# Node table of a two-layer graph network: 24 of 49 row blocks written by indirect scatters from GpSimd instead of by the sync queue's stores

## What is computed

```python
h = x @ W1 + b1                                        # layer 0
e = concatenate([h[dst], h[src] - h[dst]], axis=-1)
m = relu(relu(e @ W2 + b2) @ W3 + b3)
x = layernorm(x + relu(segment_max(m, dst, num_segments=N)))
AX = segment_sum(edge_weight[:, None] * x[src], dst, num_segments=N)   # layer 1
x = layernorm(x + AX @ W.T + b)
```

## Time and profile before

| what | value |
|---|---|
| runs | 2743.94, 2748.93, 2750.56 us |
| median | 2748.93 us |
| span of the profiled execution (first to last instruction) | 2717.3 us |
| what lies between this span and the median | 31.6 us |
| POOL busy in the span | 2132.2 us (78%) |
| TensorE busy | 1719.5 us (63%) |
| DVE, ScalarE busy | 1267.4, 1128.0 us |

### The profile page before, as it was taken

The page is one execution under the profiler, slowest core; times in us unless marked ns, Lnnn a source line. Parts: engine busy times, 40 slices in busy tenths (PEclk is TensorE's granted clock), DMA queues, the critical chain, the costliest instruction groups (busy, mean ns, idle before and its releaser), DMA issues.

```text
span 2717.3 us, 44106 instructions
## 1 busy us (share of the span) xinstructions
PE 1719.5 (63%) x9644; PEld 1460.0 (54%) x9644; DVE 1267.4 (47%) x4360; ACT 1128.0 (42%) x2966; POOL 2132.2 (78%) x1704
## 2 busy tenths in 40 slices
PE   8787777777777877455555555555555555555550
PEld 7665555555555555345555555555555555555540
DVE  6544544545445444674444444444444444444435
ACT  3555555555555555243333333333333333333323
POOL 6777777777777777568888888888888888888884
PEclk8899999999999999686666656666666666666665
DMA  5344444444444444554444444444444454444448
GB/s 157 92 126 130 127 130 129 127 128 129 128 131 127 133 125 126 160 142 52 52 53 52 52 53 53 53 52 53 52 53 53 52 53 52 52 53 53 52 42 244
DMA packets 355785, 250.40 MB, mean 92 GB/s; under 512 B 38469, under 2 KB 335009, under 8 KB 355756
## 3 DMA queue, kind: packets, MB, share of 16 engines
q0 software_dynamic: 141120, 109.29, 30.0%
q1 hardware_dynamic: 211664, 137.18, 18.3%
q10 hardware_dynamic: 2972, 3.60, 0.4%
HBM read 126.83 MB, written 123.08 MB: 92 GB/s over the span
## 4 chain that ended last, share of the span: by engine, by line
DMA 45%; POOL 27%; issue 13%; DVE 10%; PE 1%; DVEq 1%; ACT 1%; SPq 1%; POOLq 0%; ACTq 0%
DMA acc_tab<-run_e,src_idx 26%; POOL acc_tab L355 20%; DMA row_bc<-seg_row_tab 18%; DVE run L817 8%; POOL whole L320 4%; POOL whole L335 2%; POOL m L309 1%; SPq L406 0%; DVE whole L926 0%; DVE shift_by L856 0%; DVE oh L800 0%; DVE part L845 0%; DMA whole<-q_tab,src_idx 0%; DVEq L778 0%; POOL run L309 0%
## 5 line engine op out<-in xcount | busy, mean ns | idle before, releaser
L355 POOL DMA_INDIRECT acc_tab<-run_e,src_idx x784 | 1227.4, 1566 | 249.4 <-issue 166.9
L320 POOL DMA_INDIRECT whole<-q_tab,src_idx x784 | 770.6, 983 | 238.9 <-issue 234.7
L1120 PE MATMUL m_ps<-m,oh 128*128 128x128 f32 x1568 | 370.5, 411 | 614.2 <-DVE m L891 614.2
L1120 PEld LDWEIGHTS m_ps<-m,oh 128*128 128x128 f32 x1568 | 315.9, 299 | 661.7 <-DVE m L891 469.7
L908 DVE TENSOR_TENSOR src_idx<-move,src_t 128x4 int32<-128x4 f32 x196 | 33.1, 169 | 771.6 <-DMA acc_tab<-run_e,src_idx 771.4
L532 ACT ACTIVATE win_cols<-whole 128x128 f32 x1568 | 355.2, 302 | 12.7 <-issue 10.7
L608 ACT ACTIVATE m<-m_ps 128x512 f32<-128x512 f32 x196 | 117.0, 597 | 579.5 <-PE m_ps L1120 579.5
L1056 PE MATMUL m_ps<-ident,whole 128*128 128x128 f32 x1568 | 322.4, 288 | 29.6 <-DMA whole<-q_tab,src_idx 26.7
L1131 PE MATMUL z_ps<-win,m 128*128 128x128 f32 x1568 | 333.2, 384 | 1.4 <-issue 1.4
L1042 PE MATMUL s_ps<-ident,win_cols 128*128 128x128 f32 x1568 | 321.2, 343 | 10.3 <-ACT win_cols L532 10.3
L1131 PEld LDWEIGHTS z_ps<-win,m 128*128 128x128 f32 x1568 | 324.4, 305 | 1.7 <-issue 1.7
(11 more groups left out here) (173 smaller groups left out, 1807.5 us busy)
## 6 DMA issues: line engine op xcount, KB each, us to landing
seg_tab<-run_e SPq DMA_DIRECT2D x196, 256.0 KB, 2.7
row_bc<-seg_row_tab SPq DMA_DIRECT2D x196, 128.0 KB, 3.1
row_bc<-src_row_tab SPq DMA_DIRECT2D x196, 128.0 KB, 3.2
whole<-q_tab,src_idx POOLq DMA_INDIRECT x784, 3.0
acc_tab<-run_e,src_idx POOLq DMA_INDIRECT x784, 3.4
whole<-acc_tab SPq DMA_DIRECT2D x20, 512.0 KB, 6.1
acc_tab<-zeros SPq DMA_DIRECT2D x36, 256.0 KB, 3.2
q_tab<-whole SPq DMA_DIRECT2D x12, 256.0 KB
```

What stands on the lines that cost most here:

```text
L320: pool.indirect_dma_start(qg[:, r, j, :], None, q_tab[:, :], IOA(ap=src_idx[:, r, j:j + 1], axis=0)).then_inc(q_ld[r], 16)
L355: pool.indirect_dma_start(acc_tab[j][:, :], IOA(ap=src_idx[:, r, j:j + 1], axis=0), msg[:, r, j, :], None, compute_op=ALU.add).then_inc(ac ...
L1120: last = mm(m1_ps[:, s, c], lhsT=oh[:, s, c], rhs=sel[:, s, c], start=True, stop=True)
```

## The change

The first six batches of four blocks (PUT = 6) are no longer wholly SP's. POOL writes batches 0 to 3 with 16 indirect scatters of 128 rows, batch 4 with four of 64 rows (partitions 0 to 63) and batch 5 with four of 96 rows; SP stores what is left of batches 4 and 5 (64 and 32 partitions) and the batches 6 to 12 as before. The row numbers come from a new constant tile, node_row. The scatters copy, without an addition, and have a semaphore of their own, q_put. ScalarE's wait ahead of the placing and POOL's wait ahead of the gathers are now on both q_st and q_put.

```diff
+PUT = 6
+SPLITS = {4: 64, 5: 96}
...
+        node_row = sb("node_row", [P, H], I32)
...
+            nc.gpsimd.iota(node_row[:], pattern=[[P, H]], base=0, channel_multiplier=1).then_inc(rows_set, 1)
...
-            pool.wait_ge(q_st, 16 * (HX // GT))
+            pool.wait_ge(rows_set, 1)
+            for k in range(PUT):
+                pool.wait_ge(pq_sb, 2 * k + 2)
+                for h in range(k * GT, (k + 1) * GT):
+                    rows_at = IOA(ap=node_row[0:SPLITS.get(k, P), h:h + 1], axis=0)
+                    pool.indirect_dma_start(q_tab[:, :], rows_at, q_sb[0:SPLITS.get(k, P), h, :], None).then_inc(q_put, 16)
+            pool.wait_ge(q_st, 16 * (HX // GT - PUT + len(SPLITS)))
+            pool.wait_ge(q_put, 16 * PUT * GT)
...
             for k in range(HX // GT):
+                first = SPLITS.get(k, P) if k < PUT else 0
+                if first == P:
+                    continue
                 sp.wait_ge(pq_sb, 2 * k + 2)
                 b = min(H, (k + 1) * GT)
-                sp.dma_start(node(q_tab[k * GT * P:b * P, :]), q_sb[:, k * GT:b, :]).then_inc(q_st, 16)
+                sp.dma_start(node(q_tab[k * GT * P:b * P, :])[first:P], q_sb[first:P, k * GT:b, :]).then_inc(q_st, 16)
...
-            act.wait_ge(q_st, 16 * (HX // GT))
+            act.wait_ge(q_st, 16 * (HX // GT - PUT + len(SPLITS)))
+            act.wait_ge(q_put, 16 * PUT * GT)
```

More of the change, by code:

```diff
@@ L210, in gnn_kernel @@
         dve_own, counted = sem("dve_own"), sem("counted")
+        rows_set = sem("rows_set")
         pool_waited, sp_waited = sem("pool_waited"), sem("sp_waited")
@@ L219, in gnn_kernel @@
         xT_ps, xT_sb, pq_ps, pq_sb = map(sem, ("xT_ps", "xT_sb", "pq_ps", "pq_sb"))
-        q_st = sem("q_st")
+        q_st, q_put = sem("q_st"), sem("q_put")
         node_oh_done, lasts_ps, tile_found = sem("node_oh_done"), sem("lasts_ps"), sem("tile_found")
@@ L308, in _ @@
                 for h in range(CH):
+                    n = c * CH + h
                     pool.indirect_dma_start(edge_rows[k][:, h, :], None, dst_tab[:, :],
-                                            IOA(ap=tile_i[:, c * CH + h:c * CH + h + 1], axis=0)).then_inc(tile_rows[k], 16)
-            pool.wait_ge(q_st, 16 * (HX // GT))
+                                            IOA(ap=tile_i[:, n:n + 1], axis=0)).then_inc(tile_rows[k], 16)
+            pool.wait_ge(rows_set, 1)
[6 more added lines that the diff above has]
+            pool.wait_ge(q_put, 16 * PUT * GT)
             def gather(i, r):
```

## The result

| kernel | runs | median, us | ratio |
|---|---|---|---|
| before | 4 | 2747.51 (2743.94 to 2750.56) | |
| changed | 4 | 2769.81 (2764.90 to 2774.96) | 1.0083 [1.0059, 1.0107] |

The change costs 22.3 us, 16 to 29 by the interval. The direction was forecast, the size was not: 2781 was forecast with a lower end of 2773.

What follows compares the result with a forecast made beforehand. POOL's unbroken row of gathers was taken to bound layer 0. Scatters 28.75, landing 2.6 and restart 0.8 shift POOL 32.2 us, taken as 32.5; span 2749.8 plus 31.6 around it gives 2781.4 us, range 2773 to 2799.

Steps and rivals of the forecast that it cites:

- Scatters at 0.945 us in slots of 1.25: POOL, end of preparation: 24 scatters cost a plain gather's time each, so the last starts 28.75 us after 82.23.
- rival by the adding scatter's 1.55 us: POOL's scatters: each costs what the adding scatter does, 1.55 us; POOL's shift 46.8 us, time 2796; chance 0.17.
- scatters starved by DVE: POOL's scatters beside DVE's count and one-hots: seven at 2.01 us instead of 0.94 add 7.5 us, 2789; chance 0.05.
- Landing and restart, 3.4 us: Between last scatter and first gather: 2.6 us until the data lands, 0.8 us until POOL's next indirect instruction.
- ScalarE's 34.4 us: Placing on ScalarE: waits for the last scatter's landing and ends at 135.9 instead of 101.52, 34.4 us late.
- SP's relief worth nothing: SP's stores before the placing: losing four whole stores and halving two gains nothing, since neither ScalarE nor POOL waited.
- I take 32.5: End of layer 0: shift chosen between 32.2 us (gathers the bound) and 34.4 us (consumers the bound).
- win back 2.2 us: Layer 0's edge loop: consumers regain 2.2 us on POOL at 0.08 us a group, in 28 of 196 groups.
- The lead: Layer 0's edge loop: POOL's lead over the consumers was claimed to shrink by 2.2 us.
- the same 31.6 us around: Outside the profiled span: 31.6 us assumed unchanged, added to a span of 2749.8 us to give 2781.4.
- So I add nothing: DVE lengthening POOL's instructions: nothing added to the sum; two disturbed scatters, +2.1 us, allowed for the range.
- third rival: Layer 0's gathers: they get back all 30 us lost to meetings with DVE; time 2751, no change; chance 0.03.

Runs made afterwards that it cites:

- after: Profiled execution of the changed kernel, unedited, from the first comparison: span 2763.2 us, device time 2764.90 us.
- h1: The changed kernel again, unedited, against the kernel before on a chip of the faster kind: 2769.60 us against 2742.87, ratio 1.0101.
- h3: Kernel before, but SP stores only what the change leaves it and POOL scatters nothing; missing rows zero-filled early: 2743.42 us against 2742.87, ratio 0.9997.
- h4: Kernel before, but POOL pauses after 24 gathers until the placing is done: 2743.25 us against 2742.87, ratio 0.9997.
- the eight executions of the table: Profiled executions compared by first gather, first maximum, mean gather, last gather and TensorE idle: h1, h2, h3, h4, k1, k2, after, and before as first profiled.
- k2: Kernel before with one more wait on ScalarE ahead of the placing, POOL not delayed, faster kind of chip: 2742.48 us against 2736.64, ratio 1.0016.
- h2: Kernel before plus 24 POOL scatters of zeros to an unread table; SP stores all, ScalarE waits for SP alone: 2782.47 us against 2742.87, ratio 1.0147.
- k1: Kernel before with the running maximum's second input read from PSUM, faster kind of chip: 2707.40 us against 2736.64, ratio 0.9889.
- e3: Kernel before with the running maximum's second input read from PSUM, slower kind of chip: 3107.07 us against 3097.55, ratio 1.0037.
- g3: Repeat of e3 on another job's chip, again of the slower kind: 3125.12 us against 3126.81, ratio 0.9994.

## Why the prediction was right and wrong

- **Scatters at 0.945 us in slots of 1.25:** right. 28.9 us for 28.75; the full ones 0.02 to 0.05 us dearer, the partial ones 0.04 cheaper. The rival by the adding scatter's 1.55 us is refuted, and so is that of scatters starved by DVE: none took over 1.01 us in the profiles of after and h1. The Trainium skill's trap (page SBUF — State Buffer, "SBUF: two separate sides") did not strike where I looked for it, in the scatters. A hold-up of its kind strikes the gathers of the loop, up to 1.0 us each, and by an operation with two SBUF inputs, where the trap as stated there speaks of a mode with two ports.
- **Landing and restart, 3.4 us:** 2.98. From the scatters' first start to the first gather are 31.9 us; the prediction had 32.2. In the five executions of the old preparation the first gather starts at 80.1 to 82.6, and in the three of the new one at 112.8 to 113.1.
- **ScalarE's 34.4 us:** 32.4, without the stall. **SP's relief worth nothing:** right, 0.9997 in h3.
- **The step that failed is the sum:** "I take 32.5", built on gathers whose mean stays at 980, so on a hold-up that the change leaves alone, and on consumers that win back 2.2 us. Measured were 22.3 (16 to 29) and 26.7 (22 to 33). POOL's 32 us arrive at the first gather, and a part is given back inside the loop. The last gather ends at 1134.8 and 1136.7 against 1105.4 and 1108.2 (h1 and after against h4 and h3): 29 us, not 32. The hold-up is 42 and 45 us against 45 and 49, 3 us less on average, and this is the whole of the difference. These 29 us are still there at the last maximum (1147.2 and 1145.9 against 1116.7 and 1118.2), and 29 lies inside both intervals. That the medians are 2 and 7 us below it is not explained; from the last maximum to the end the eight executions of the table take 1615.7 to 1621.4 us without a pattern, a spread of the same size. The lower end of the range, 2773, stands for +24.1: the first comparison lies below it by 2 us, the second above it by 3.
- **The lead:** the prediction has it the wrong way round. Consumers shifted by 34.4 us and gathers by 32.2 make POOL's lead longer, not shorter; it is 34.0 and 36.4 us against 32.1 and 32.2. A longer lead goes with less hold-up in k2 (66 us of lead, 35 us of hold-up), and without ScalarE's later start the cost is 39.6 (h2). That the 2 to 4 us by which the change itself widens the lead are what takes 3 us off the hold-up is only argued; two executions of each kernel cannot show it. In the table's extremes 16 us of lead go with 273.8 us of idle time and 66 us with 3.2.
- **The base:** the profile of before was of an execution some 25 us faster than the usual. Its mean of 983 ns was taken as the kernel's, when the usual mean is 1002 to 1007. Setting the sum on the median of the runs kept most of this out of the number, but "the same 31.6 us around" was wrong as a statement: no run shows more than 3.8. The expected end of the last gather, 1124, was missed by 13 us. The consumers' win-back of 0.08 us a group came from that execution as well; in h4 the consumers take 5.02 us a group and POOL 5.1 to 5.2 until they fall into step.
- **"So I add nothing"** for DVE was right for the scatters and left the loop fixed. The third rival (gathers get back their disturbance) named the true mechanism. That its price, 30 us, is near k1's gain of 29.2 is luck: the 30 us came from the unusual execution, the usual hold-up is 45, and k1 won 29 of it because the other engines are the bound from there on. The rival was taken as all or nothing with a chance of 0.03; with the 3 us that the profiles show the lower end of the range would have been 2770.

**What stays open:** why h2 costs more than POOL's 31.9 us (its profiled execution, 2770.1, was 12 us below its own median, and its last gather ends 33 us later than before); what makes the execution of the first profile meet the maximum less often at a lead of 32 us; what stops the engines on the slower kind of chip, whether it is the chip at all or something that changes with time, and why e3 is 9.5 us slower there when g3 is not. The changed kernel with the PSUM operand ran on the slower kind alone.

## What to carry to other kernels

Work added to an engine that has no hole moves all that stands behind it by its whole row of slots. How much of that reaches the time is decided by what the engines lose to each other later: here 22 to 27 us of 32 in the change, 40 with POOL's part alone. When the busy engine's mean duration lies above its undisturbed one, find the instruction that overlaps the long ones first: here moving one operand of it into PSUM was worth more than the change cost. Compare the profiled span with the timed runs before setting a sum on it: in one execution span and time lie 1.7 to 3.8 us apart here, so a distance of 1% means that the profile is of an unusual execution.

## What was not expected of the hardware

- A running maximum with two SBUF inputs holds up GpSimd's descriptor work until it ends, by up to 1.0 us (392 of 393 gathers that start 0.08 to 0.87 us into it); with one of the inputs in PSUM it does not (0 of 129). The Trainium skill (SBUF — State Buffer, "SBUF: two separate sides") states a lock on a port that GpSimd and DVE share, and lets a DVE operation with two SBUF inputs take it only against a GpSimd operation that reads SBUF. The trace agrees with the lock, by the 0.75 us left after each end, and shows that making the descriptors of a gather counts among what it stops.
- An indirect scatter of 64 rows costs GpSimd 0.90 us and one of 128 rows 0.97: splitting by rows buys next to nothing.
- The same kernel takes 2737 to 2749 us on some chips and 3098 to 3129 on others, and what pays on one kind (k1, -29.2 us) pays nothing on the other (e3 +9.5, g3 -1.7).
